# Cross-attention similarities of a decoder layer: one fp32 product against three products of split parts

## The reference

```
scores = einsum('bsr,nr->bsn', Q, K) / sqrt(128)          # 8192 keys
topk_scores, topk_idx = top_k(scores, 8)
output = einsum('bskd,bsk->bsd', V[topk_idx], softmax(topk_scores))
...
q, k, v = heads(x @ Wq), heads(context @ Wk), heads(context @ Wv)   # 16 heads of 64
sim = clip(where(mask, q k^T * 64**-0.5, -big), -5, 5)
out = (softmax(sim) @ v) @ Wo + bo
```

## Time and profile before

| | |
|---|---|
| median of 3 runs | 1410.86 us (1408.49 to 1416.77) |
| profiled execution, its own time | 1410.62 us |
| its span | 1408.8 us |
| PE busy | 1328.3 us, 94% |
| DVE busy | 1090.9 us, 77% |
| ACT busy | 726.7 us, 52% |
| POOL busy | 721.5 us, 51% |
| granted TensorE clock, mean | 0.969 of 2.4 GHz |

### The profile page before, as it was taken

One profiled execution on the slowest core, in us unless ns is written; L12 is line 12 of the kernel. 1 busy time (PEld: TensorE's weight loads), 2 busy tenths in 40 slices (PEclk: granted clock), 3 DMA queues, 4 the chain that ended last, 5 costly groups with the idle time before them and its releaser, 6 DMA issues.

```text
span 1408.8 us, 25227 instructions
## 1 busy us (share of the span) xinstructions
PE 1328.3 (94%) x9853; PEld 999.4 (71%) x9853; DVE 1090.9 (77%) x1627; ACT 726.7 (52%) x1377; POOL 721.5 (51%) x1009
## 2 busy tenths in 40 slices
PE   9765699999999999999999999999999988999898
PEld 5444577777777787878686868686868675877665
DVE  1459999888888888888888888979797865255557
ACT  1353465555565646464646464656565543435455
POOL 0524456555565656464646474747474753340434
PEclk7877899999999999999999999999999999999999
DMA  9451212121212121212122222222221340021412
GB/s 370 165 187 35 81 45 74 53 73 54 72 54 72 53 72 53 73 54 76 58 71 68 61 69 64 69 57 73 55 69 47 87 143 17 15 61 47 152 39 84
DMA packets 57021, 109.85 MB, mean 78 GB/s; under 512 B 9422, under 2 KB 37574, under 8 KB 55750
## 3 DMA queue, kind: packets, MB, share of 16 engines
q1 hardware_dynamic: 39814, 61.64, 14.4%
q0 software_dynamic: 14848, 41.96, 10.2%
q10 hardware_dynamic: 2240, 4.63, 0.9%
HBM read 98.24 MB, written 9.95 MB: 77 GB/s over the span
## 4 chain that ended last, share of the span: by engine, by line
PE 84%; DVE 9%; issue 2%; POOL 2%; DMA 1%; ACT 1%; SPq 1%; POOLq 0%; DVEq 0%; ACTq 0%
PE side_bank L379 49%; PE score_bank L379 31%; DVE cand_val L1112 2%; DVE cand_idx L1113 2%; PE score_bank L732 2%; DVE x_sum L1136 1%; POOL v_rows L1330 1%; PE side_bank L732 1%; POOL exp L1359 1%; DMA sc_in<-shared_compress 1%; DVE dispatchedT L1268 1%; PE side_bank L530 0%; PE score_bank L588 0%; DMA shared_compress<-xT_by_step 0%; DVE pos_onehot L1123 0%
## 5 line engine op out<-in xcount | busy, mean ns | idle before, releaser
L877 ACT COPY score_row<-score_bank 128x512 f32<-128x512 f32 x512 | 298.7, 588 | 174.3 <-PE score_bank L379 100.1
L1112 DVE MAX8 cand_val<-score_row 128x8 f32<-128x2048 f32 x128 | 292.2, 2283 | 103.4 <-ACT score_row L877 103.4
L1330 POOL DMA_INDIRECT v_rows<-in_V,top_idx x256 | 248.1, 969 | 188.6 <-DVE top_idx L1126 106.3
L1359 POOL TENSOR_SCALAR exp<-exp,exp_bound 128x256 f32<-128x256 f32 x512 | 243.0, 490 | 125.9 <-ACT exp L889 125.3
L1113 DVE FIND_INDEX8 cand_idx<-cand_val,score_row 128x8 uint32<-128x2048 f32 x128 | 292.5, 2285 | 0.0
L379 PE MATMUL score_bank<-keysT_hi,qT_hi 128*128 128x512 f32 x512 | 218.6, 427 | 30.7 <-ACT score_row L877 29.6
L379 PE MATMUL score_bank<-keysT_lo,qT_hi 128*128 128x512 f32 x512 | 205.3, 401 | 0.0
L379 PE MATMUL score_bank<-keysT_hi,qT_lo 128*128 128x512 f32 x512 | 205.1, 401 | 0.0
L889 ACT ACTIVATE exp<-side_bank 128x512 f32<-128x512 f32 x256 | 139.0, 595 | 86.8 <-PE side_bank L379 86.8
L379 PEld LDWEIGHTS score_bank<-keysT_hi,qT_hi 128*128 128x128 f32 x512 | 98.2, 192 | 69.4 <-ACT score_row L877 34.5
L379 PE MATMUL side_bank<-qT_heads,kT 64*128 64x256 f32 x1024 | 145.2, 402 | 0.0
(11 more groups left out here) (200 smaller groups left out, 2296.5 us busy)
## 6 DMA issues: line engine op xcount, KB each, us to landing
kT<-den_scratch SPq DMA_DIRECT2D x62, 256.0 KB, 3.9
f_quads<-in_f POOLq DMA_DIRECT2D x32, 256.0 KB, 3.6
comp_then_wqkv_raw<-in_comp SPq DMA_DIRECT2D x6, 1024.0 KB, 18.2
xT_by_step<-in_xTs SPq DMA_DIRECT2D x4, 1024.0 KB, 9.3
keysT_raw<-in_KmT ACTq DMA_DIRECT2D x8, 512.0 KB, 13.4
xT_in<-in_xT SPq DMA_DIRECT2D x16, 256.0 KB, 3.8
x_sum<-in_x SPq DMA_DIRECT2D x32, 128.0 KB, 2.1
ctxT_in<-in_ctxT SPq DMA_DIRECT2D x16, 256.0 KB, 4.6
```

The lines of the kernel that those rows point to most:

```text
L877: nc.scalar.copy(srow[n // PER % 2][:, i * CB:(i + 1) * CB], scb[n % 3]).then_inc(sem("score_evac"), 1)
L1112: own(nc.vector.max(cv[:, tile, cs], srow[g % 2][:, :]))
L1330: pool.indirect_dma_start(out=vg[:, k, :], out_offset=None, in_=V_rows, in_offset=bass.IndirectOffsetOnAxis(ap=i8[:, tile, k:k + 1], axis=0))\
L1359: last = nc.gpsimd.tensor_scalar(ex[i % NEX][:, k, :], ex[i % NEX][:, k, :], ub[:, k, c:c + 1], E_LO, ALU.min, ALU.max)
```

## The change

- The similarities of a pair of heads are computed with `mm3`'s three products, each for the two heads: twelve fp32r matmuls of 256 columns and 64 rows in place of four fp32 ones.
- Keys: ScalarE writes the high part of K and a raw copy (two copies in place of one), GpSimd subtracts (`keys_lo`, in place in the raw buffer). Queries: ScalarE writes the high part, VectorE subtracts out of the bank (`queries_lo`) and frees it. The low parts have two buffers each of a quarter of the heads; they, the high parts and the old kT and qT_heads share memory.
- To make room, `NEX` goes from 10 to 6, and `denominators` is called four times a turn, for four heads each, after every `values`.
- Projections K2, Q2 and K3, Q3 move from the first half of the turn to places behind `sims(c, 1)` and `sims(c, 3)`; so the order of jobs is K0 K1 WO WO Q0 Q1 q K2 Q2 PV0 K3 Q3 PV1 PV2 PV3 V0 to V3.
- VectorE's list: the first `residual2` stands ahead of search 0, the second between its MAX8 and FIND_INDEX8; the four `queries_lo` stand between the searches, and searches 1 to 4 each stand one place of other work later.
- GpSimd's list: `keys_lo` 0 and 1 at the head of the turn, 2 and 3 behind the clips of heads 3 and 7; the low part of the context moves from head 5 to head 9.

```diff
-NEX = 10
+NEX = 6
...
     if cross:
-        jobs += [("K", c, j) for j in range(4)]
+        jobs += [("K", c, 0), ("K", c, 1)]
...
-        jobs += [("Q", c, j) for j in range(4)]
+        jobs += [("Q", c, 0), ("Q", c, 1)]
...
-        jobs += [("PV", c, j) for j in range(NP // 2)]
+        jobs += [("K", c, 2), ("Q", c, 2), ("PV", c, 0), ("K", c, 3), ("Q", c, 3), ("PV", c, 1), ("PV", c, 2), ("PV", c, 3)]
...
             def sims(c, p):
                 if p % 2 == 0:
-                    job_done(pe, ("K", c, p // 2))
+                    need(pe, "kT_lo", 4 * c + p // 2 + 1)
                     job_done(pe, ("Q", c, p // 2))
                 need(pe, "exp_done", H * c + 2 * p)
+                kl_, ql = klo[p // 2 % 2], qlo[p // 2 % 2]
                 for k in range(KT):
-                    for o in range(2):
-                        r = slice(64 * o, 64 * o + 64)
-                        last = mm(sp_[o][:, k * S:(k + 1) * S], kt[r, p, k * P:(k + 1) * P], qt[r, p, :])
+                    kc = slice(k * P, (k + 1) * P)
+                    for n, (left, right) in enumerate(((khi[:, p, kc], qhi[:, p, :]), (khi[:, p, kc], ql[:, p % 2, :]),
+                                                       (kl_[:, p % 2, kc], qhi[:, p, :]))):
+                        for o in range(2):
+                            r = slice(64 * o, 64 * o + 64)
+                            last = mm(sp_[o][:, k * S:(k + 1) * S], left[r, :], right[r, :], start=(n == 0), stop=(n == 2))
...
                     if cross and j:
                         values(c, j - 1)
-                        if j == 2:
-                            denominators(c, 0)
+                        denominators(c, j - 1)
                     if cross:
                         sims(c, 2 * j + 1)
                     select(c, 2 * j + 1)
+                    if cross and j < 2:
+                        project(("K", c, j + 2), 1, 2 * (j + 2) * P, cth, ctl)
+                        project(("Q", c, j + 2), 0, 2 * (j + 2) * P, x1h, x1l)
                     for e in range(4):
                         score(c, 12 + 4 * j + e)
...
+            def keys_out(c, j):
+
+                key, ns = ("K", c, j), slice(2 * j, 2 * j + 2)
+                need(act, "ot_done", 2 * (c - 1) + 1 + j // 2)
+                job_full(act, key)
+                nc.scalar.copy(khi[:, ns, :].rearrange("p a s -> p (a s)"), job_bank(key)[:, :])
+                nc.scalar.copy(kraw_heads[j % 2][:, :, :].rearrange("p a s -> p (a s)"), job_bank(key)[:, :])\
+                    .then_inc(free(key), 1)
...
+            def queries_lo(c, j):
...
+                need(dve, "heads_q_hi", 4 * c + j + 1)
+                if j >= 2:
+                    need(dve, "sim_full", NP * c + 2 * (j - 2) + 2)
+                nc.vector.tensor_tensor(qlo[j % 2][:, :, :].rearrange("p a s -> p (a s)"), job_bank(key)[:, :],
+                                        qhi[:, 2 * j:2 * j + 2, :].bitcast(F32).rearrange("p a s -> p (a s)"),
+                                        ALU.subtract).then_inc(free(key), 1)
...
+            def keys_lo(c, j):
+                job_done(pool, ("K", c, j))
+                nc.gpsimd.tensor_tensor(klo[j % 2][:, :, :], kraw_heads[j % 2][:, :, :],
+                                        khi[:, 2 * j:2 * j + 2, :].bitcast(F32), ALU.subtract).then_inc(sem("kT_lo"), 1)
```

More of the change, by code:

```diff
@@ L202, in build @@
         cth, ctl = sb(work, "ctx_hi", [P, KT, S], F32R), sb(work, "ctx_lo", [P, KT, S], F32R)
+        split = work.enter_context(ExitStack())
+        khi = sb(split, "kT_hi", [P, NP, S], F32R)
+        qhi = sb(split, "qT_heads_hi", [P, NP, S], F32R)
+        kraw_heads = [sb(split, f"kT_raw{i}", [P, 2, S]) for i in range(2)]
+        split.close()
         kt = sb(work, "kT", [P, NP, S])
         qt = sb(work, "qT_heads", [P, NP, S])
+        klo = [sb(work, f"kT_lo{i}", [P, 2, S], F32R) for i in range(2)]
+        qlo = [sb(work, f"qT_heads_lo{i}", [P, 2, S], F32R) for i in range(2)]
         vv = sb(work, "v", [P, KT, INNER])
@@ L560, in values, with denominators @@
                 last.then_inc(full(key), 1)
-            def denominators(c, h):
-                need(pe, "rden_done", 2 * c + h)
-                for j in range(2):
-                    for k in range(KT):
-                        for q in range(4):
-                            last = mm(den[32 * q:32 * q + 32, :], sel[:, j, :],
-                                      ex[(H * c + 8 * h + 4 * j + q) % NEX][:, k, :],
-                                      start=(j == 0 and k == 0), stop=(j == 1 and k == KT - 1))
+            def denominators(c, j):
+                if j % 2 == 0:
+                    need(pe, "rden_done", 2 * c + j // 2)
+                for k in range(KT):
+                    for q in range(4):
+                        last = mm(den[32 * q:32 * q + 32, :], sel[:, j % 2, :], ex[(H * c + 4 * j + q) % NEX][:, k, :],
+                                  start=(j % 2 == 0 and k == 0), stop=(j % 2 == 1 and k == KT - 1))
                 last.then_inc(sem("den_full"), 1)
@@ L611, in _ @@
                     need(pe, "ctx_lo", c + 1)
-                for j in range(4):
+                for j in range(2):
                     if cross:
                         project(("K", c, j), 1, 2 * j * P, cth, ctl)
-                    score(c, j)
+                    score(c, 2 * j)
+                    score(c, 2 * j + 1)
                 for tile in range(TT):
@@ L629, in _ @@
                     need(pe, "x1_lo", TT * (c + 1))
-                for j in range(4):
-                    if cross and j == 3:
-                        sims(c, 0)
+                for j in range(2):
                     if cross:
@@ L635, in _ @@
                     score(c, 8 + j)
+                score(c, 10)
+                if cross:
+                    sims(c, 0)
                 if prep:
                     shared_q(a + 1)
+                score(c, 11)
                 for j in range(NP // 2):
@@ L652, in _ @@
                     values(c, NP // 2 - 1)
-                    denominators(c, 1)
+                    denominators(c, NP // 2 - 1)
                 if mid:
@@ L934, in _ @@
                     select(c, 2 * j + 1)
+                    if cross and j < 2:
+                        keys_out(c, j + 2)
+                        queries_hi(c, j + 2)
                     for e in range(4):
@@ L1205, in _ @@
                     residual2(p, 0, z)
+                candidates(c, 0, p)
+                queries_lo(c, 0)
                 if mid:
                     merge(m, 1)
-                if out:
-                    residual2(p, 1, z)
-                candidates(c, 1)
+                queries_lo(c, 1)
                 if out:
@@ L1229, in _ @@
                     value_sum(m, 1, range(TOPK))
-                candidates(c, 4)
+                queries_lo(c, 3)
+                candidates(c, 3)
                 select(c, (2, 3))
@@ L1361, in _ @@
                         last.then_inc(sem("clip_done"), 1)
+                    if cross and h in (3, 7):
+                        keys_lo(c, 2 + h // 4)
                     if cross and m < B - 1 and h == 1:
```

63 lines of the change are left out of this document (39 added, 24 removed).

## The result

| | before | after |
|---|---|---|
| median of the runs, same chip | 1412.01 us (1408.49 to 1416.77, 4 runs) | 1487.71 us (1481.19 to 1491.46, 4 runs) |
| profiled execution, its own time | 1410.62 us | 1481.19 us |
| its span | 1408.8 us | 1478.8 us |
| PE, DVE, ACT, POOL busy | 1328.3, 1090.9, 726.7, 721.5 us | 1337.9, 1170.3, 747.1, 809.5 us |
| a turn, mean of turns 1 to 12 | 68.53 us | 72.33 us |

The account below looks back on a forecast made before the run. TensorE was taken to bound the kernel; turns 1 to 12 at -0.88 + 1.7 + 0.6 = +1.4 us each (+17.0), turn 13 +1.4 and ends +5.0 put +23.4 on 1410.62 us: 1434, range 1403 to 1450.

Parts of the forecast that it names:

- Part 1, the products: Similarities on TensorE: a block takes 0.92 us against 1.06, for eight blocks -1.18 us a turn.
- The rival by the rule on loads: Similarities: the two heads' fp32r loads do not overlap, twelve steps in place of six, 4.5 us a turn, 1492; chance 0.07.
- Part 2, denominators: Denominators on TensorE: a block has about 0.15 us of its own, two blocks more a turn, +0.30.
- Part 3, hidden copies: ScalarE's four key copies (2.4 us a turn) and GpSimd's four low parts (5.1) fit beside 31 and 29 us free.
- Part 4, Q2 behind the low part of q: Q2 needs the bank VectorE frees: TensorE ready at 8.7 us, VectorE at 10.4, wait 1.7 (0.7 to 2.7).
- Part 5, block 23 behind search 3: Search 3 stands behind tile 1's value-row sum: ready at 32.8 us, TensorE at 32.2, wait 0.6 (0 to 2.0).
- nothing in them looks blocked: VectorE's eight value-row additions, 4.54 us beside GpSimd's clips before the change; blocking by GpSimd left out of the sum.
- The sum: Turns 1 to 12 +1.4 us each (+17.0), turn 13 +1.4, ends +5.0: +23.4 us, 1434.
- the ends: Start-up +2.2 us, turn 0 +3.3 (0 to 6), turn 14 +0.2, turn 15 -0.7; together +5.0.
- The argument of the second wait bounding the turn by itself: Block 23's wait would be 1.7 us longer without the wait at Q2, so it alone bounds the turn.
- The rival that VectorE becomes the bound: GpSimd holds VectorE's instructions, TensorE waits at score 20 to 31, 1.3 us more a turn: 1452; chance 0.06.
- The three other rivals: Low part of q in time, 1399 (0.18); waits eat the gain, 1410 (0.16); pair not a pair, 1492 (0.07).

Follow-up runs that it names:

- e9: e8 with one plain fp32 product for the similarities in place of the three fp32r ones, read from the high parts alone: 1429.92 us, ratio 1.0091.
- e7: Kernel before, with only the softmax denominators in four calls of four heads a turn in place of two of eight: 1417.35 us, ratio 1.0032.
- e11: Changed kernel with one move, GpSimd's low part of K3 behind the clips of head 8 in place of head 7: 1464.27 us, ratio 1.0334.
- e2: Changed kernel with search 3 ahead of the sum of the value rows of tile 1, as in the kernel before: 1447.69 us, ratio 1.0256.
- e8: e5 plus K3's low part behind head 8's clips, q's early only with cross-attention, turn 0's first queries' low part ahead of search 0: 1410.17 us, ratio 0.9981.
- e1: Changed kernel with VectorE's low part of q ahead of search 1 in place of behind it: 1520.8 us, ratio 1.0755.
- e5: Changed kernel with the moves of e1 and e2, and GpSimd's gathers issued three, one and four in place of five, one and two: 1437.46 us, ratio 1.0169.
- e15: The kernel of e8 unchanged, run a third time: 1412.31 us, ratio 0.9988.
- e13: The kernel of e8 unchanged, run again in another series: 1419.92 us, ratio 1.0031.

## Why the prediction was wrong, step by step

- **Part 1, the products: right.** A block 0.91 us (0.92 forecast), the pair a pair in fp32r; e9 prices the difference at 0.16. The rival by the rule on loads is out.
- **Part 2, denominators: right** (+0.28 by e7, +0.30 forecast). Together TensorE's own work fell by 0.99 a turn (-0.88 forecast).
- **Part 3, hidden copies: wrong in what "hidden" was taken to mean.** ScalarE's four copies hid. GpSimd's four low parts had their free time as counted, but they held VectorE. The only direct price is the low part of K3, 23 to 27 us in all (e11).
- **Part 4, Q2 behind the low part of q: the wait was right, its cost was not.** In turn 4 the low part ended 10.6 us after Q0 (10.4 forecast), and TensorE waited 1.88 (1.7). What the step left out is what comes behind a wait: in e2 a turn with it is 69.7 - 67.5 = 2.1 longer at full clock and 3.7 longer when the clock falls, nine turns in twelve.
- **Part 5, block 23 behind search 3: the failed step.** In turn 4, counted from Q0's end, the last gather ended at 19.8 (19.5), its rows were there at 21.8 (21.6; the assumed 2.1 for the landing was good), and from there to search 3 it took 7.2 - 0.6 = 6.6 where 5.3 stood. The 1.3 more are one addition of 1.84 us and others of 0.58, beside clips and kT_lo. The prediction counted kT_lo of K2 as the danger, found it early enough, and did not ask the same of kT_lo of K3, which stands behind the clips of head 7, where the additions are. VectorE's side was 1.7 us later than counted, 1.3 of it by this, TensorE was 0.5 later, and so the wait was 1.8 in place of 0.6. With that one instruction moved away it was 0.56 to 0.61 (e11). The sum went by "nothing in them looks blocked", but those eight at 0.57 from start to start are longer than the 0.52 of undisturbed ones (655.00 and the next in the chain above: 0.50 and the step between): clips held them a little already, and no instruction of 1.28 us ran beside them.
- **The sum.** Turns 1 to 12 are 3.80 us longer in the mean, not 1.4: 29 us of the 47 by which the profiled execution (1481.2) passed 1434; the other 18 are at the ends. In the shortest turns: -0.99, two waits of 1.88 and 1.78, and 0.26 for each new start behind one (2.14 in e2's 69.68 - 67.54, less 1.88) make +3.2, that is 71.7. Of the 1.8 between that and the forecast of +1.4, block 23 is 1.2, what a new start costs 0.5 and Q2 0.2, less 0.1 of TensorE's own work. The rest are four turns of 72.9 to 75.1 us with longer waits (2.3 and 2.5 ahead of Q2 in turns 2 and 5, 2.5, 1.6 and 3.0 ahead of block 23 in turns 2, 9 and 11) and a fall of the clock in all but turn 11. Turn 13 was +6.8 (+1.4 forecast), with 3.7 us ahead of block 23; turn 0 was +9.5 (+3.3), with waits of 4.7 and 1.9 us and a mean clock of 0.93; turn 14 was +2.9 (+0.2), what follows it +3.1 (-0.7); the start-up was +2.2 as forecast, which says little: e7, with the start-up of the kernel before, has its first transpose at 178.2 us and the kernel before at 172.9.
- **The argument of the second wait bounding the turn by itself was right, and its consequence was not drawn.** If a loop through VectorE and GpSimd sets the turn, each held instruction in it counts in full. The rival that VectorE becomes the bound named that mechanism with 0.06 and 1.3 us a turn; it had the right mechanism, and block 23 is among its score blocks 20 to 31. But it had VectorE short of time as a whole, where VectorE was late on one path (e8 leaves it 2.9 us free a turn), and its 1452 was still 29 us below the profiled 1481.2. Its chance was too low. The three other rivals are out.

## What to carry to other kernels

When work is moved to an engine that has free time, look at what the other engine does beside it in each place where it now stands (here GpSimd beside VectorE's instructions with two SBUF inputs), and cost the meeting on the path of the one that waits. Of a new wait on TensorE, cost also the slower clock behind it: here 1.5 us for a wait of 1.9, in nine turns of twelve. And where two waits follow each other in a loop, take the later one out first: moving one search (e2) gave some 40 us, taking out the earlier wait (e1) lost some 33.

## What was not expected of the hardware

- A VectorE addition of 0.48 us took 3.23 us while GpSimd went through its list without a gap, and a 128x8 instruction 2.63 us (e1, e5). In both it went on only at or near the end of GpSimd's row of instructions. In turn 6 of the changed kernel additions and clips alternated instead, at 0.58 and 0.65 us, and why the two differ is open.
- The granted clock fell to its lower level behind nine of twelve waits of only 1.9 us that look alike (e2), 0.3 to 1.3 us after TensorE had started again, and cost 1.5 us each time.
- Loads of 64 rows for two heads overlap in fp32r as in fp32: six pairs of steps of 0.12 us.
- The same kernel had turns of 67.54 us in two of the series of runs (e8, e15) and of 68.2 in another (e13), with a pause of ScalarE whose releaser the profile does not name.
